# Second units at every fourth pair of layer 0, and a fourth early panel, in a two-layer graph kernel

## What is computed

```
# layer 0
A' = a*A, and (1-a) added on its diagonal
x0 = relu((A' / A'.sum(axis=1)) @ x @ W.T + b)
x  = layernorm(x + x0)
# layer 1
t     = logmap0(x)
par   = adj   * sigmoid(t@w_par[:d][:,None] + t@w_par[d:][None,:] + b_par)
chi   = adj.T * sigmoid(t@w_chi[:d][:,None] + t@w_chi[d:][None,:] + b_chi)
s     = chi @ t + par @ t
x     = layernorm(x + proj(expmap0(s)))
```

## Time and profile before

| | us |
|---|---|
| median of 3 runs | 2200.4 |
| lowest and highest | 2196.5, 2200.65 |
| profiled execution, own time | 2200.13 |
| its span | 2198.3 |

### The profile page before, as it was taken

One profiled execution on the slowest core, in us unless ns is written; L12 is line 12 of the kernel. 1 busy time (PEld: TensorE's weight loads), 2 busy tenths in 40 slices (PEclk: granted clock), 3 DMA queues, 4 the chain that ended last, 5 costly groups with the idle time before them and its releaser, 6 DMA issues. The chain is left out here.

```text
span 2198.3 us, 18369 instructions
## 1 busy us (share of the span) xinstructions
PE 2006.2 (91%) x5072; PEld 898.4 (41%) x5072; DVE 1929.8 (88%) x1864; ACT 1318.0 (60%) x1508; POOL 1340.4 (61%) x639
## 2 busy tenths in 40 slices
PE   7999999999999998999999978898888888889886
PEld 3444444444444444444444433343333333334333
DVE  5757787988989989898999989999998998989896
ACT  0001324454464454454453588988989988989996
POOL 0000304534455554644544677999998998999996
PEclk9999999999999999999999988999999999999998
DMA  9978988989989989988989998999999999999993
GB/s 338 362 273 291 400 288 349 406 343 384 388 329 409 414 331 363 392 337 337 416 345 348 422 408 329 421 420 421 422 410 421 421 419 394 421 421 398 398 393 143
DMA packets 128453, 820.37 MB, mean 373 GB/s; under 512 B 14880, under 2 KB 27488, under 8 KB 31328
## 3 DMA queue, kind: packets, MB, share of 16 engines
q1 hardware_dynamic: 113392, 799.06, 90.7%
q10 hardware_dynamic: 14960, 20.13, 2.7%
HBM read 814.88 MB, written 4.26 MB: 373 GB/s over the span
## 5 line engine op out<-in xcount | busy, mean ns | idle before, releaser
L548 POOL TENSOR_TENSOR chi<-chi,ring 128x1024 f32<-128x1024 f32 x326 | 834.4, 2573 | 628.5 <-ACT chi L756 572.4
L1244 PE MATMUL ps<-keys,xtA 128*128 128x512 f32 x2048 | 981.3, 611 | 140.1 <-DVE keys L1045 110.5
L1171 PE MATMUL ps<-ring,xA 128*128 128x512 f32 x2048 | 918.4, 598 | 33.8 <-DMA xA<-in_x_g 15.2
L773 ACT ACTIVATE ps<-scores,prcr 128x1024 f32<-128x1024 f32 x492 | 544.2, 1106 | 394.2 <-DVE keys L1045 377.5
L1244 PEld LDWEIGHTS ps<-keys,xtA 128*128 128x128 f32 x2048 | 377.6, 193 | 683.8 <-issue 653.0
L935 DVE TENSOR_TENSOR dsum<-dsum,ring 128x2048 f32<-128x2048 f32 x240 | 594.1, 2475 | 30.4 <-DMA ring<-in_g_blk 24.4
L1171 PEld LDWEIGHTS ps<-ring,xA 128*128 128x128 f32 x2048 | 387.5, 192 | 519.1 <-issue 493.9
L1045 DVE TENSOR_TENSOR keys<-ps,chi 128x1024 f32<-128x1024 f32 x426 | 521.6, 1225 | 85.6 <-issue 31.3
L756 ACT ACTIVATE chi<-scores,prcr 128x1024 f32<-128x1024 f32 x426 | 483.8, 1136 | 16.3 <-DMA scores<-plcl_d 8.5
L1036 DVE TENSOR_TENSOR ps<-ps,ring 128x1024 f32<-128x1024 f32 x348 | 425.5, 1223 | 44.4 <-ACT ps L773 39.0
L548 POOL TENSOR_TENSOR chi<-chi,xA 128x1024 f32<-128x1024 f32 x79 | 185.7, 2366 | 18.4 <-ACT chi L756 18.4
(11 more groups left out here) (122 smaller groups left out, 820.9 us busy)
## 6 DMA issues: line engine op xcount, KB each, us to landing
ring<-in_g_blk SPq DMA_DIRECT2D x443, 1024.0 KB, 8.6
ring<-in_a_cols SPq DMA_DIRECT2D x190, 1024.0 KB, 10.0
xA<-in_a_cols SPq DMA_DIRECT2D x51, 1024.0 KB, 11.9
xA<-in_g_blk SPq DMA_DIRECT2D x44, 1024.0 KB, 10.0
scores<-in_a_cols SPq DMA_DIRECT2D x15, 1024.0 KB, 11.7
scores<-in_g_blk SPq DMA_DIRECT2D x15, 1024.0 KB, 10.7
scores<-plcl_d ACTq DMA_DIRECT2D x22, 512.0 KB, 10.4
xA<-in_x_g ACTq DMA_DIRECT2D x64, 64.0 KB, 11.8
```

Of the source, the lines that this page charges most:

```text
L548: pool.tensor_tensor(out=chi(n), in0=chi(n), in1=half(t, n), op=ALU.mult).then_inc(m2_ready, 1)
L773: act.activation(dst, scores[:, row, 0, :], ACT.Sigmoid, bias=prcr[:, 2 * jt:2 * jt + 1]).then_inc(p_ready, 1)
L1171: ins = pe.matmul(Y[:, h * BANK:(h + 1) * BANK], xA[:, tile * D:(tile + 1) * D], t[:, tt * BP + h * BANK:tt * BP + (h + 1) * BANK], start= ...
L1244: ins = pe.matmul(outp[:, h * BANK:(h + 1) * BANK], xtA[:, jt * D:(jt + 1) * D], keys(n)[:, h * BANK:(h + 1) * BANK], start=begins, stop=i ...
```

## The change

EARLY goes from 3 to 4, so four panels have a partial sum in `acc` and units among the pairs; the order of the early groups is given by a small table for input panels 4 and 6. From pair DENSE = 118 on, every pair whose number is a multiple of 4 takes two units. 204 units instead of 154 are issued among the pairs: the gaps at 206-213 and 238-245 are filled, and 34 pairs (120, 124, ... 252) have two. In such a pair DVE does the degree sum in two halves of 128 x 1024, around the first unit's first product and key; only in the first pair of a panel (q < 2) the sum stays whole. `taken` loses its own buffer and lies in the not yet written last panel of `xtA` (the last one in `xA`); the third row buffer, which was a ring entry in the late part, becomes a fourth and fifth chi buffer and the own-block buffer. Row buffers are reloaded when a panel comes that isn't in one. In the late part the closing work of panels comes every 26 to 28 units for seven of the eight.

```diff
-EARLY = 3
+EARLY = 4
+CB_MORE = 2
...
+EARLY_ORDER = {4: (3, 2, 1, 0), 6: (2, 3, 1, 0)}
+ENDS_BEHIND = {4: (0, 1), 5: (2, 3)}
...
-        for p in range(min(EARLY, a + 1)):
+        for p in EARLY_ORDER.get(a, range(min(EARLY, a + 1))):
...
+DENSE = (EARLY - 1) * PPP + T_UNITS
...
     for g in range(PAIRS):
-        if waiting and waiting[0][3] <= g:
-            k, p, jt, _ = waiting.pop(0)
-            unit_at[g] = len(units)
-            units.append((k, p, jt))
+        for _ in range(2 if g >= DENSE and g % 4 == 0 else 1):
+            if waiting and waiting[0][3] <= g:
+                k, p, jt, _ = waiting.pop(0)
+                unit_at.setdefault(g, []).append(len(units))
+                units.append((k, p, jt))
...
-        if k - EARLY < EARLY:
-            order.append((k - EARLY, range((NPAN - 1) * TPP, UPP)))
+        for p in ENDS_BEHIND.get(k, ()):
+            order.append((p, range((NPAN - 1) * TPP, UPP)))
...
-            out.append((p - EARLY, base[p] + 34))
+        for i, q in enumerate(ENDS_BEHIND.get(p, ())):
+            out.append((q, base[p] + 28 + 26 * i))
...
-        if kind == "nat" and 2 * j == (ENDS[ROWS_GONE] + 16) // 2 * 2:
-            entries.insert(0, RING + EXTRA)
...
-        own_par = [taken[:, :], xA[:, EXTRA * CH + BP:EXTRA * CH + 2 * BP]]
+        own_par = [scores[:, 2, 0, :], xA[:, EXTRA * CH + BP:EXTRA * CH + 2 * BP]]
+        def taken(k):
+            return own_par[1] if k in TAKEN_LATE else xtA[:, (NPAN - 1) * BP:N]
...
+            def degree_sums_half(g, i):
+                t, here, count = loaded("pair", g)
+                if i == 0:
+                    dve.wait_ge(here, count)
+                    dve.wait_ge(deg_added, g)
+                ins = dve.tensor_tensor(out=half(dsum, i), in0=half(dsum, i), in1=half(t, i), op=ALU.add)
+                if i == 1:
+                    ins.then_inc(deg_added, 1)
...
-                degree_sums(g)
+                if len(units) == 2 and q >= 2:
+                    degree_sums_half(g, 0)
+                    first_product(units[0])
+                    key(units[0])
+                    degree_sums_half(g, 1)
+                else:
+                    degree_sums(g)
+                    for n in units[:-1]:
+                        first_product(n)
+                        key(n)
                 if r > 0:
                     passage(r - 1, q)
-                if g in UNIT_AT:
-                    first_product(UNIT_AT[g])
+                if units:
+                    first_product(units[-1])
...
-                if g - PE_LAG in UNIT_AT:
-                    products(UNIT_AT[g - PE_LAG])
+                for n in UNIT_AT.get(g - PE_LAG, ()):
+                    products(n)
```

More of the change, by code:

```diff
@@ L179 @@
 SLOT_OF_UNIT, SLOT_OF_NORMS, SLOT_OF_FINAL = slot_plan()
-ROWS_GONE = max(k for k, (p, _, a) in enumerate(GROUPS) if p == 2 and a < NPAN - 1)
 def load_plan():
@@ L190, in load_plan @@
         kinds.append(("pair", g))
-        if g in UNIT_AT and UNIT_AT[g] % 2 == 0:
-            kinds += [("nat", UNIT_AT[g] // 2), ("trn", UNIT_AT[g] // 2)]
+        for n in UNIT_AT.get(g, ()):
+            if n % 2 == 0:
+                kinds += [("nat", n // 2), ("trn", n // 2)]
     late = len(kinds)
@@ L219, in row_plan @@
 def row_plan():
-    out, use, end_of = {}, [0, 0, 0], [None, None, None]
-    buf = 0
+    out, use, holder, end_of = {}, [0, 0, 0], [None, None, None], [None, None, None]
+    late = 0
     for k, (p, tiles, a) in enumerate(GROUPS):
         if a < NPAN - 1:
[L224 to L227, removed]
-        else:
-            b = buf % 2
-            buf += 1
+            b = p % 3
+        else:
+            late += 1
+            b = late % 2
+        fetched = None
+        if holder[b] != p:
             use[b] += 1
-            out[k] = (b, use[b], end_of[b])
-        end_of[b] = ENDS[k]
+            fetched = end_of[b]
+        out[k] = (b, use[b], fetched)
+        holder[b], end_of[b] = p, ENDS[k]
     return out
@@ L240, in rows_of @@
 def rows_of(n):
-    k, p, _ = UNIT[n]
-    return ROWS_OF[(p, "early")] if GROUPS[k][2] < NPAN - 1 else ROWS_OF[k]
+    return ROWS_OF[UNIT[n][0]]
 def evac_plan():
-    pair_of = {n: g for g, n in UNIT_AT.items()}
+    pair_of = {n: g for g, both in UNIT_AT.items() for n in both}
     at_pair, at_unit = {}, {}
@@ L265, with chi_buffer @@
 ADDED_ALL = ADDED[-1]
+TAKEN_LATE = [k for n, k in EVAC_AT_UNIT.items() if n >= LATE0 + 16]
+ADDED_BEFORE_TANGENT = ADDED[min(TAKEN_LATE)]
 ROW_LOAD_AT = {}
 for _k, (_p, _t, _a) in enumerate(GROUPS):
-    if _a == NPAN - 1:
+    if ROWS_OF[_k][2] is not None:
         ROW_LOAD_AT.setdefault(ROWS_OF[_k][2] + 2, []).append(_k)
-MORE = LATE0 + 16
-def buffer_of(n, few):
+ROWS_GONE = max(k for k, (p, _, a) in enumerate(GROUPS) if p == 2 and a < NPAN - 1)
+MORE = max(ENDS[ROWS_GONE] + 8, LATE0 + 16)
+def chi_buffer(n):
     if n < MORE:
-        return n % few, n - few if n >= few else None
-    k = (n - MORE) % (few + 1)
-    return (few, n - few - 1 if n > MORE else None) if k == 0 else ((MORE + k - 1) % few, n - few - 1)
+        return n % CB, n - CB if n >= CB else None
+    k = (n - MORE) % (CB + CB_MORE)
+    before = n - CB - CB_MORE
+    return (CB + k, before if before >= MORE else None) if k < CB_MORE else ((MORE + k - CB_MORE) % CB, before)
 APART = {n for n in range(MORE + 8, UNITS) if n % 8 == 2 and n not in OWN_AT}
@@ L393, in adj_resnorm_kernel @@
         x_in = [sem(f"x_in{G}") for G in range(NG)]
-        r_in = [sem(f"r_in{e}") for e in range(RING + EXTRA + 1)]
+        r_in = [sem(f"r_in{e}") for e in range(RING + EXTRA)]
         l_in = [sem(f"l_in{k}") for k in range(3)]
@@ L556, in add_taken @@
                 pool.wait_ge(out_evac, k + 1)
-                pool.tensor_tensor(out=at, in0=taken[:, :], in1=at, op=ALU.add).then_inc(acc_added, 1)
+                pool.tensor_tensor(out=at, in0=taken(k), in1=at, op=ALU.add).then_inc(acc_added, 1)
             def norm_floor(k):
@@ L626, in _ @@
                     fold(r - 1)
-                if g in UNIT_AT:
-                    second_product(UNIT_AT[g])
+                for n in UNIT_AT.get(g, ()):
+                    second_product(n)
                 if g in EVAC_AT_PAIR:
@@ L738, in passage @@
                     copy_rows(r)
-                if tick == T_LOADL and r < EARLY:
+                if tick == T_LOADL and r < 3:
                     load_rows(r, r)
@@ L747, in sigmoids @@
                 act.wait_ge(prcr_ready, jt // TPP + 1)
-                b, before = buffer_of(n, CB)
+                b, before = chi_buffer(n)
                 if before in APART:
@@ L1289, in _ @@
                 pair(g)
-                if g - PE_LAG in UNIT_AT:
-                    products(UNIT_AT[g - PE_LAG])
+                for n in UNIT_AT.get(g - PE_LAG, ()):
+                    products(n)
             for g in range(PAIRS - PE_LAG, PAIRS):
-                if g in UNIT_AT:
-                    products(UNIT_AT[g])
+                for n in UNIT_AT.get(g, ()):
+                    products(n)
             for n in range(N_EARLY, UNITS):
```

41 lines of the change are left out of this document (22 added, 19 removed).

## The result

The changed kernel takes 2243.2 us (median of four runs, 2240.6 to 2246.7) against 2199.1 for the kernel before: the ratio is 1.0203, 95% interval 1.0183 to 1.0223. It is 44 us slower, where 2193 had been forecast with a range up to 2228.

What follows compares the result with a forecast made beforehand. TensorE bounds the pairs from 118 on, DMA the late part; with the change DVE becomes slowest among the pairs. 2200.1 - 116 (late part) + 109 (pairs) = 2193 us, range 2158 to 2228.

Steps and rivals of the forecast that it cites:

- The late part: After layer 0: 50 units fewer at 2.516 us each, less added loads, saves 116 us.
- Where it is decided: Pairs from 118 on: DVE passes TensorE as the engine with most work, 804 against 800.5 us before lock waits.
- The wait: Doubled pairs: the second half sum stands behind POOL's product, thirty times 1.13 us, 34 us.
- The rule that the prediction took from the Trainium skill: DVE instructions with two SBUF inputs and GpSimd instructions reading SBUF exclude each other; the later stands still. No size.
- I take 39 - 15 = +24 us net: Pairs from 118 on: new waits on DVE add 39 us, old lock waits shrink by 15; range 0 to +55.
- I take 2%: Pairs from 118 on: DVE idles 2%, so 828 us of work takes 845 us.
- The slower one: Pairs 124 to 252: every second half stands 1.13 us behind POOL, old waits stay; 2218 us, chance 0.30.
- Late loads: Among the pairs: ring entries come free a load too late, 42 us on top, 2235 us; chance 0.06.
- the sign that the prediction named for being wrong: Layer 0: DMA waits ahead of matmuls in the tens of microseconds would show the forecast wrong.
- That TensorE stays the limit: Pairs from 118 on: DVE's work hides under TensorE's 800.5 us; +89 there, 2173 us, chance 0.22.

Runs made afterwards that it cites:

- e9: The changed kernel with the second half sum of the 30 doubled pairs left out, so half of their degrees is missing: 2238.1 us.
- e11: The changed kernel with POOL's products made to wait for the degree sum, a second unit's for the second half sum: 2268.1 us.
- e1: The changed kernel with an eighth ring entry for loads issued from pair 114 to pair 195: 2241.0 us.
- e12: The changed kernel with POOL's second products among the pairs replaced by constant writes about as long, reading no SBUF: 2177.3 us.
- e5: The changed kernel with POOL's second products among the pairs replaced by one shorter constant write, reading no SBUF: 2173.0 us.
- e6: The kernel before with POOL's second products among the pairs replaced by one shorter constant write, reading no SBUF: 2167.7 us.
- e13: The kernel before with POOL's second products among the pairs replaced by constant writes about as long, reading no SBUF: 2169.5 us.

## Why the prediction was wrong, point by point

**The late part** was right: -116 forecast, -119.0 measured, and 266 second products in 680 us (late part of the changed kernel, 1510 to 2190) are 2.56 us a unit, where 2.516 had been counted.

```profile
1510.00:2190.00 680.00, 619.17 (x266) 0.99 1.00 410
```

**Where it is decided** was right in the main: DVE has more busy time than TensorE (846 against 823 us), and the second halves stand. The wait was computed to 1.13 us from a single pair's timeline and measured 0.86 on 30 of 30, 26 us where 34 had been computed. The rule that the prediction took from the Trainium skill (SBUF — State Buffer, section on who interferes with whom) held here too: the sum at 964.91 ended at 968.45, and POOL's end at 966.30 plus 2.28 is 968.58. But this wait is not the mechanism by itself: taking it away gained 5 us (e9) or lost 25 (e11), while taking away the reads of all of POOL's products among the pairs gained 66.

**The failed step is the one behind it**, "I take 39 - 15 = +24 us net". The old lock waits did not shrink by 15, they grew. Sums and halves in the stretch stand (2.821 - 2.28) x 99 + (1.743 - 1.22) x 60 = 54 + 31 = 85 us, where sums stood 36: +49, twice the term. The halves' 31 are about what had been computed; it is the whole sums, fewer than before, that stand 54 instead of 36. What was overlooked is that a collision reaches into the next pair: of the 30 sums in the pair behind a split one 26 stand, 0.70 us on average, where sums stood 0.28 before. And an addition into `acc` behind a product meets the sum that this product held up. It was late in 11 of 14 cases, where it had been in 2 of 11 (line 571, has its undisturbed 2.35):

```profile
L571 POOL TENSOR_TENSOR acc<-xtA,acc x17: 2354/4400/4413, 398.8 to 1455.1; 128x1024 f32<-128x1024 f32 x17
```

One such chain, in pair 166, DVE and then POOL:

```profile
808.96 3.40 DVE L957 TENSOR_TENSOR dsum<-dsum,ring 128x2048 f32<-128x2048 f32 x1
814.68 4.37 DVE L957 TENSOR_TENSOR dsum<-dsum,ring 128x2048 f32<-128x2048 f32 x1
...
807.85 2.36 POOL L562 TENSOR_TENSOR chi<-chi,ring 128x1024 f32<-128x1024 f32 x1 [2.29 <-ACT chi L775]
810.17 4.41 POOL L571 TENSOR_TENSOR acc<-xtA,acc 128x1024 f32<-128x1024 f32 x1
814.54 2.37 POOL L562 TENSOR_TENSOR chi<-chi,ring 128x1024 f32<-128x1024 f32 x1
```

The sum at 808.96 stands behind the product, the addition behind that sum, and the next product, now late, ahead of the next sum. DVE's busy time came out 18 us over the forecast (846.1 against 828): the other 7 of the 25 us between +49 and +24 came back elsewhere, where four small instructions of the passage that had stood 1.9 us each no longer did.

**The second failed step is the idle share**, "I take 2%". DVE idled 896.1 - 846.1 = 50 us, 5.6%, not 17. The 3% had come from the one stretch of the earlier trace rows that holds no step of the passage on DVE; over all five rows it was 7.5%, 55 us, and that hardly shrank: DVE's waits for the sigmoid (11.1 us before, 18.6 after) and for POOL (10.4 and 9.3) stay when DVE becomes the slowest, since they are part of its own chain and not slack. 18 + 33 is the whole of the 51 us by which the stretch was missed.

Behind both steps is that one limit with one idle share was taken for the whole stretch. At places 0 to 7 TensorE set the time, and at place 8, in the thick of the passage, neither did: in the row of pair 168 above, TensorE is busy 25.0 and DVE 30.3 of 32.9 us.

**The rivals.** The slower one had the place and let the old waits stay; its 2218 was short by the same two terms. Late loads had the size by chance (2235) and the cause wrong, as e1 and e12 show; the sign that the prediction named for being wrong, waits for DMA in the tens of microseconds, did come (48.2), but as a consequence. That TensorE stays the limit holds only where POOL's products don't read (e12), and even there the stretch costs 129 us more and not 89, so the change is no gain.

**The rest of the 44 us.** 8 us, give or take 5, remain without the lock. There the 50 units cost 837.2 - 708.3 = 129 us, 2.6 each and not TensorE's 1.71: 98 us are TensorE's busy time, the other 31 its waits, for loads and for take-outs. Which of these come with the doubled pairs and which with more groups was not taken apart. Nor was it shown why gaps and doubled pairs add up as they do: 39 us for 16 units and 121 for 34 (3.6 each), with 18 and 101 given back.

No version here that computes the whole result beats the kernel before. e5, e6, e12 and e13 say what one would have to do: the lock alone costs it some 31 us of 2199.

## What to carry to other kernels

Filling an engine's idle time with work that the trace shows to be cheap elsewhere pays only if the engine that has least slack there has any; here moving a unit from a place where it cost 2.5 us made it cost 3.2, though TensorE's own price is 1.71. Idle time of the next engine in line is not slack until it is shown what ends it: when it is the engine's own chain, it comes along at full length.

Where two engines exclude each other, count the collisions over a whole cycle of pairs, not of the one instruction that is moved; a blocked instruction makes the next one late, and that one meets the following. And to find what such an exclusion costs, replace the one side by work of the same length that doesn't touch the shared thing, in both kernels.

## What the runs showed of the hardware that had not been expected

Taking the reads away from POOL's products, at equal length, made the kernel before 31 us faster (2169.5 against 2200.1, ratio 0.986) and the changed one 66 us. DVE's busy time in the stretch fell by 49 us before (680.3 to 631.7) and by 98 after (846.1 to 748.5), so about two thirds of what DVE stood came back as time in both kernels, even in the one before, in which TensorE is busy 97% of the stretch. POOL's own standing went with it (0.43 us a product before, 0.23 after), and these runs don't tell the two apart.

The lengths of DVE's sums in the trace include the standing, so an engine that is blocked in this way counts as busy there. It is not only the large instructions that stand: in the kernel before, a step of the passage with 8 elements a partition (128x8, `small<-mv,small`) took 2.08 us on average, and 0.17 in e13.
